# Four row slots a stage, rows addressed by byte offset and shared by SyncE and ScalarE, attribute loads issued by ScalarE

## The chip, the cores and the metric

The kernel runs on one core of a Trainium2 chip. The metric is device time in microseconds of one execution. The kernel before has a median of 3977.24 us in three runs (3971.26 to 3994.51).

## What is computed

The graph has 6250 nodes with 128 features, and 100000 directed edges sorted by target (`dst`). Two blocks follow each other, each added to its own input; each begins with a layer norm and a ReLU over the node features. The first block is two layers with edge attributes, the second two layers without:

```
h = relu(layernorm(x))                         # before each block
# block 1, two layers:
msg = relu(x[src] + edge_attr)                 # 100000 x 128
agg = segment_sum(msg, dst)                    # 6250 x 128
h = (x + agg) @ W1 + b1;  h = batchnorm(h) * gamma + beta
x = relu(relu(h) @ W2 + b2)
# block 2, two layers:
agg = segment_sum(x[src], dst)
x = relu((x + agg) @ wA + bA) @ wB + bB        # relu between the layers
```

## The kernel before, in words

Edges are handled 512 at a time, 4 per partition (`EPP`); such a group is a slot. Four slots make a turn, 49 turns (`TURNS`) a pass over all edges. Each of the four layers is one pass, called a stage here. The change touches the first two stages, those with edge attributes, and leaves the other two alone.

In a turn of the first two stages:

- **GpSimd** gathers node rows. For each slot it issues 4 indirect DMAs (line 629), each of 128 rows of the node table in HBM into one of two gather buffers `xg`. It may fill a buffer again when VectorE has summed the slots of two turns ago.
- **SyncE** issues, in this order (`edges`, line 534): the stores of finished count units (line 538, after ScalarE's cast of the unit), then, once TensorE is done with the turn, the edge attributes of the turn three ahead (1 MB in two DMAs, lines 499 and 503, into a ring of three), then `gather_rows`.
- **`gather_rows`** (line 507) is a second way of fetching node rows. Slot 2 of turns 25 and 48 isn't gathered by GpSimd; its 512 rows are fetched singly by SyncE into the tile `row_slot`. Six partitions of 4 rows each, 24 rows, are fetched in a turn: turns 2 to 23 for the first of these slots, 26 to 47 for the second. A load of 4 indices into registers (line 520) is followed by 4 DMAs of one table row, 512 bytes (line 524), each with register operations for its address. The index is a row number.
- **ScalarE** copies one attribute slot at a time to a bank of PSUM, `ea_stage` (line 704), turns sums into messages with a ReLU, two slots at a time (line 709), and casts finished count units to `count_out` (line 696), two of which are in flight to HBM.
- **VectorE** adds the gathered rows to the staged attributes (`slot_sum`, line 1048), which frees the bank for ScalarE's next copy. Between these sums it builds one-hot rows of the chunks of edges to be counted (`cell_room`, line 1035), once a turn the one-hot windows of targets (`hid`, line 995), and it adds TensorE's window sums to `acc` (line 948).
- **TensorE** first builds the counts of the turn (line 1407) and then sums messages into windows, 32 matmuls a turn (line 1423), whose last one increments `scattered`.

The counts built in the first two stages serve the last two, which need no attributes. The order of all of it is written out by hand, each engine having its own program, in which it runs strictly in order; semaphores tie them. In the code, `layer` is the stage, `n` the turn over both stages (0 to 97), `u` the slot.

Of the kernel before, what the change touches and what calls it, by code (L numbers as in the profile page):

```python
# [14 lines left out]
BF16 = mybir.dt.bfloat16  # L15

P = 128
NODES = 6250
EDGES = 100000
D = 128  # L20
EPP = 4
# [4 lines left out]
SLOTS = 4  # L26
# [68 lines left out]
ROW_TURNS = (25, TURNS - 1)  # L95
ROW_STARTS = (2, 26)
ROW_STEP = 6
# [21 lines left out]
def units_in(chunks):  # L119

    return [UNIT_OF[e] for c in chunks for e in (2 * c, 2 * c + 1) if e + 1 in UNIT_END]

# [59 lines left out]
def gnn_kernel(nc, x, src, dst, edge_attr, W1, b1, gamma, beta, W2, b2,  # L182
               w1a, b1a, w1b, b1b, eps1, w2a, b2a, w2b, b2b, eps2, out):
    with ExitStack() as ctx:
# [102 lines left out]
        row_slot = sb("row_slot", [P, EPP * D])  # L287
        product = row_slot[:, 0:UPG * CW].rearrange("p (s c) -> p s c", s=UPG)
# [90 lines left out]
        gathered = [[sem(f"gathered{q}_{u}") for u in range(SLOTS)] for q in range(2)]  # L379
        row_landed = [sem(f"row_landed{k}") for k in range(len(ROW_TURNS))]  # L380
# [48 lines left out]
        def load_plan(eng):  # L429

            eng.wait_ge(plan_ready, 2)
            return (eng.value_load(plan_i[0:1, 1:2], min_val=0, max_val=SKIP),
                    eng.value_load(plan_i[0:1, 2:3], min_val=LEFT_PAIRS, max_val=TURNS // 2),
                    eng.value_load(plan_i[0:1, 3:4], min_val=0, max_val=1))

# [24 lines left out]
        def _(sp):  # L460
# [32 lines left out]

            def load_turn(n):

                k, t = n % TURNS, n % RING
                e0 = k * SLOTS * SUP
                most = SLOTS - 1
                sp.dma_start(ea[:, t, 0:most, :, :].rearrange("p u j d -> p u (j d)"),  # L499
                             edge_attr[e0:e0 + most * SUP, :].rearrange("(u p j) d -> p u (j d)", p=P, j=EPP)  # L500
                             ).then_inc(ea_loaded[t], 16)
                e1 = min(e0 + most * SUP, TAIL_START)
                sp.dma_start(ea[:, t, most, :, :].rearrange("p j d -> p (j d)"),  # L503
                             edge_attr[e1:e1 + SUP, :].rearrange("(p j) d -> p (j d)", j=EPP)
                             ).then_inc(ea_loaded[t], 16)

            def gather_rows(layer, t):

                for k, (first, used) in enumerate(zip(ROW_STARTS, ROW_TURNS)):
                    p0 = (t - first) * ROW_STEP  # L510
                    if not 0 <= p0 < P:
                        continue
                    if t == first:
                        sp.wait_ge(table_written, 16 * GROUPS * (layer + 1))
                        if layer or k:
                            last = (layer * TURNS + ROW_TURNS[k - 1] - (0 if k else TURNS)) * SLOTS + ROW_SLOT
                            sp.wait_ge(summed, last + 1)
                    s = used * SLOTS + ROW_SLOT
# [15 lines left out]
            def edges(layer):  # L534
                for n in range(layer * TURNS, (layer + 1) * TURNS):
# [32 lines left out]
            rounds = load_rounds(sp)  # L568
            edges(0)
# [91 lines left out]
        def _(act):  # L661
# [36 lines left out]

            def stage_attributes(i):

                n, u = divmod(i, SLOTS)
                if u == 0:
                    act.wait_ge(ea_loaded[n % RING], 32 * (n // RING + 1))
                act.copy(ea_stage, ea[:, n % RING, u, :, :].rearrange("p j d -> p (j d)")).then_inc(ea_staged, 1)  # L704

# [5 lines left out]
            def edges(layer):  # L711
                start = RAW_TURNS if layer == 0 else layer * TURNS
                for n in range(layer * TURNS, start):
                    for slots in HALVES:
                        act.wait_ge(summed, n * SLOTS + slots[-1] + 1)
                        messages(n, slots)
                act.wait_ge(windows_cleared, 2 * (layer + 1))
                stage_attributes(start * SLOTS)
                for n in range(start, (layer + 1) * TURNS):
                    for slots in HALVES:  # L720
                        for u in slots:
# [4 lines left out]
                            if u == slots[-1]:  # L726
                                messages(n, slots)
                            units_out(slot_chunks(n, u))

# [108 lines left out]
            act.wait_ge(params_loaded, PARAMS)  # L838
            for layer in range(LAYERS):
                if layer < 2:  # L840
                    edges(layer)
                else:
                    if layer == 2:
                        rounds = load_rounds(act)
# [10 lines left out]
        def _(dve):  # L855
# [183 lines left out]
            def slot_sum(n, u):  # L1039
# [3 lines left out]
                if by_rows(n, u):  # L1043
                    k, rows = ROW_TURNS.index(n % TURNS), row_slot[:, :]
# [583 lines left out]
```

## Time and profile before

| | |
|---|---|
| median of 3 runs | 3977.24 us |
| profiled execution, own time | 4016.24 us |
| its span | 4014.3 us |
| granted TensorE clock, mean | 0.733 |
| busy share: TensorE, VectorE, ScalarE, GpSimd | 53%, 42%, 18%, 48% |
| first stage, turns 5 to 48 by SyncE's count | about 163 to 1509 us |
| second stage, row turns | about 1687 to 2958 us |
| third and fourth stage | about 3045 to 4014 us |

The span is that of the instructions; the execution's own time has 2 us more around it. A busy share is an average over stages with different limits. A wait that ends by "issue" is one in which the engine waited for nothing that the profile shows. "remote" is a releaser that the profile could not name.

### The profile page before, as it was taken

To read this page: it belongs to the slowest core of one execution; us is meant where nothing else is said; L and a number is where in the kernel's file an instruction comes from. 1 tells how busy PE (TensorE), PEld (TensorE's weight loads), DVE (VectorE), ACT (ScalarE), POOL (GpSimd) and SP (SyncE) were. 2 spreads that over 40 slices of the span, in tenths; PEclk is the share of its full clock that TensorE was granted. 3 is DMA by queue.
4 is the path that set the end of the run, shared out by engine and by line. 5 is a ranking of instruction groups with operands and counts; after the bars stand their busy time and mean duration, and the time that the engine had idled before them with its cause. 6 is when DMAs were issued, how large, how long until landed. Compare 5 with 4: busy or idle time off the path is not lost.

```text
span 4014.3 us, 37448 instructions
## 1 busy us (share of the span) xinstructions
PE 2131.0 (53%) x9399; PEld 1315.4 (33%) x9399; DVE 1694.4 (42%) x2879; ACT 732.8 (18%) x1002; POOL 1944.6 (48%) x2048
## 2 busy tenths in 40 slices
PE   2454544444444454344434454353456887877878
PEld 1332323332232232222222232232233444444445
DVE  6554435445454443445445554444456111151112
ACT  3111112121111123122112222222234000020001
POOL 5555445455453523655554554455423455445552
PEclk8676666766666677666766776666767898888889
DMA  4222222222222232232332323333323444443442
GB/s 141 72 74 76 84 62 79 78 89 82 73 81 74 82 89 84 75 89 82 101 100 87 108 90 108 91 93 97 113 83 106 151 147 134 132 143 124 151 148 83
DMA packets 228500, 396.97 MB, mean 99 GB/s; under 512 B 43017, under 2 KB 132957, under 8 KB 228325
## 3 DMA queue, kind: packets, MB, share of 16 engines
q1 hardware_dynamic: 163300, 261.77, 19.8%
q0 software_dynamic: 65024, 133.30, 13.0%
q8 instruction: 57, 0.93, 0.1%
q14 instruction: 119, 0.97, 0.1%
HBM read 333.10 MB, written 61.81 MB: 98 GB/s over the span
## 4 chain that ended last, share of the span: by engine, by line
SPq 38%; issue 30%; PE 21%; another core or an unknown queue 6%; DVE 4%; ACT 1%; DMA 0%; DVEq 0%; ACTq 0%
SPq L524 28%; PE psA L1450 13%; SPq L520 6%; PE psG L1465 4%; SPq L503 1%; PE psG L1514 1%; SPq L499 1%; PE psG L1423 1%; SPq L538 1%; PE psA L1522 1%; DVE cell_room L1035 0%; DVE rows_h L902 0%; PE psA L1407 0%; PE psG L1544 0%
## 5 line engine op out<-in xcount | busy, mean ns | idle before, releaser
L629 POOL DMA_INDIRECT xg<-node_table,src_all x1520 | 1441.7, 948 | 1457.7 <-DVE xp_room L1048 891.0
L1407 PE MATMUL psA<-cell_room,xp_room 128*128 128x512 f16 (+1 forms) x2336 | 705.8, 452 | 1061.9 <-ACT count_out L696 621.0
L1423 PE MATMUL psG<-hid,xp_room 128*128 128x160 f32 x3072 | 582.5, 352 | 487.4 <-issue 278.9
L1035 DVE TENSOR_SCALAR cell_room<-psG,cell_all 128x932 f16<-128x932 int16 x1088 | 686.5, 690 | 199.9 <-remote 158.0
L1407 PEld LDWEIGHTS psA<-cell_room,xp_room 128*128 128x128 f16 x2336 | 258.9, 115 | 1492.2 <-issue 682.1
L1048 DVE TENSOR_TENSOR xp_room<-psG,xg 128x512 f32<-128x512 f32 x380 | 258.0, 679 | 1117.7 <-ACT psG L704 992.3
L649 POOL DMA_INDIRECT xg<-node_table,idx x480 | 469.0, 977 | 535.3 <-issue 380.2
L1423 PEld LDWEIGHTS psG<-hid,xp_room 128*128 128x128 f32 x3072 | 547.1, 233 | 520.1 <-issue 380.8
L704 ACT COPY psG<-xp_room 128x512 f32<-128x512 f32 x384 | 226.5, 590 | 1230.5 <-DMA xp_room<-in_edge_attr_dram 627.2
L696 ACT CAST count_out<-psA 128x1862 f16<-128x1862 f32 x96 | 164.2, 1710 | 1061.2 <-DMA count_store<-count_out 444.1
L1450 PE MATMUL psA<-cell_room,xp_room 128*128 128x456 f16 x1200 | 275.2, 383 | 99.6 <-issue 77.7
L948 DVE TENSOR_TENSOR acc<-acc,row_slot 128x38 f32 x192 | 38.6, 201 | 632.7 <-ACT row_slot L756 526.7
L995 DVE SCALAR_TENSOR_TENSOR hid<-loc_all,round_off,psG 128x2560 f32<-128x2560 f32 x96 | 274.7, 2861 | 0.0
L1450 PE MATMUL psA<-hid,xp_room 128*128 128x456 f16 x1152 | 240.2, 368 | 15.0 <-issue 15.0
L1465 PE MATMUL psG<-rows_h,xg 128*128 128x160 f32 x960 | 193.7, 356 | 80.4 <-issue 80.3
L1465 PEld LDWEIGHTS psG<-rows_h,xg 128*128 128x128 f32 x960 | 177.2, 236 | 101.3 <-issue 99.2
L709 ACT ACTIVATE xp_room<-xp_room 128x1024 f32<-128x1024 f32 x196 | 206.2, 1053 | 9.7 <-issue 7.2
L1450 PEld LDWEIGHTS psA<-cell_room,xp_room 128*128 128x128 bf16 x1200 | 120.7, 101 | 246.6 <-issue 145.3
L948 DVE TENSOR_TENSOR acc<-acc,psG 128x160 f32 x272 | 86.9, 319 | 185.5 <-issue 89.9
L756 ACT COPY row_slot<-psA 128x456 f32<-128x456 f32 x16 | 8.6, 539 | 831.9 <-remote 695.0
L1450 PEld LDWEIGHTS psA<-hid,xp_room 128*128 128x128 bf16 x1152 | 112.3, 98 | 138.3 <-issue 22.6
L1014 DVE TENSOR_TENSOR xp_room<-psG,src_lo_all 128x768 f16<-128x768 int16 (+2 forms) x132 | 93.2, 727 | 0.0
(154 smaller groups left out, 824.4 us busy)
## 6 DMA issues: line engine op xcount, KB each, us to landing
xp_room<-in_edge_attr_dram SPq DMA_DIRECT2D x98, 768.0 KB
cell_room<-count_store SPq DMA_DIRECT2D x16, 2850.0 KB
count_store<-count_out SPq DMA_DIRECT2D x96, 465.5 KB
hid<-count_store SPq DMA_DIRECT2D x16, 2736.0 KB
row_slot<-node_table SPq DMA_DIRECT2D x2048, 0.5 KB
xp_room<-in_edge_attr_dram SPq DMA_DIRECT2D x98, 256.0 KB
xg<-node_table,src_all POOLq DMA_INDIRECT x1520
node_table<-rows_h SPq DMA_DIRECT2D x48, 256.0 KB
```

Source lines behind the costliest of these rows:

```text
L520: _, rows = nc.values_load_multi_w_load_instructions(src_all[p:p + 1, s, :], [mybir.EngineType.SP], min_val=0, max_val=NODES - 1, skip_run ...
L524: sp.dma_start(row_slot[p:p + 1, j * D:(j + 1) * D], table[bass.DynSlice(row, 1), :]).then_inc(row_landed[k], 16)
L629: nc.gpsimd.indirect_dma_start(xg[:, n % 2, u, j, :], None, x if n < RAW_TURNS else table, bass.IndirectOffsetOnAxis(ap=src_all[:, s, j:j ...
L649: nc.gpsimd.indirect_dma_start(xg[:, q, u, j, :], None, table, bass.IndirectOffsetOnAxis(ap=idx[:, q, u, j:j + 1], axis=0),).then_inc(row_ ...
L704: act.copy(ea_stage, ea[:, n % RING, u, :, :].rearrange("p j d -> p (j d)")).then_inc(ea_staged, 1)
L995: nc.vector.scalar_tensor_tensor(out=rows.rearrange("p u j w -> p (u j) w"), in0=loc.unsqueeze(2).broadcast_to((P, SLOTS * EPP, WIN)), sca ...
L1035: nc.vector.tensor_scalar(cells[:, c % CELL_RING, c0:c1], iota_bank[:, 0:c1 - c0], float(c0), cell_all[:, c:c + 1], ALU.add, ALU.is_equal) ...
L1048: nc.vector.tensor_tensor(ea[:, n % RING, u, :, :].rearrange("p j d -> p (j d)"), ea_stage, rows, ALU.add).then_inc(summed, 1)
L1407: last = nc.tensor.matmul(psA[:, bank, 0:w], src_hot[:, hots(n) % 2, at, :], cells[:, c % CELL_RING, c0:c0 + w], start=first, stop=end)
L1423: last = nc.tensor.matmul(psG[:, q, h * WIN:(h + 1) * WIN], ea[:, t, u, j, :], rows[:, u, j, :], start=(u == slots[0] and j == 0), stop=(u ...
L1450: last = nc.tensor.matmul(out_cols, xp[:, b, part, :], counts[h][:, :, i * CW:(i + 1) * CW], start=(b == 0 and part == 0), stop=(b == BLOC ...
L1465: last = nc.tensor.matmul(psG[:, q, h * WIN:(h + 1) * WIN], xg[:, q, u, j, :], late_hot[:, q, u * EPP + j, :], start=(u == slots[0] and j ...
```

## The change

- Four slots of each of the first two stages come row by row: slot 2 of turns 15, 26, 37 and 48. They go alternately into `row_slot` and into the last 512 columns of `hid`, which the one-hot windows don't reach.
- The 512 partition groups of 4 rows are worked off at 12 groups a turn, from turn 3 on: 8 groups (32 rows) by SyncE, 4 groups (16 rows) by ScalarE.
- The indices of these slots are loaded once, at the start, into the tile `idx` (free until the third stage), and shifted left by 9 bits by VectorE: they are byte offsets into the table, which is viewed as bytes. One index load of SyncE covers up to 4 groups (16 values), one of ScalarE 2 groups (8 values).
- ScalarE loads indices behind slots 0 and 2 of a turn and issues 4 rows behind each of the four slots.
- The attribute load of turn n + 2 (the ring's next) is issued by ScalarE, behind slot 1 of turn n and its first messages, after a wait for TensorE's windows of turn n - 1. SyncE no longer waits for TensorE in these stages.

```diff
-ROW_TURNS = (25, TURNS - 1)
-ROW_STARTS = (2, 26)
-ROW_STEP = 6
+ROW_TURNS = (15, 26, 37, TURNS - 1)
+ROW_START = 3
+BY_SYNC = 8
+ACT_GROUPS = ((1, 1), (1, 1))
+BY_ACT = sum(map(sum, ACT_GROUPS))
+ROW_STEP = BY_SYNC + BY_ACT
+ROW_LOAD = 4
...
+def row_work(t):
+    first = (t - ROW_START) * ROW_STEP
+    return [divmod(i, P) for i in range(first, first + ROW_STEP) if 0 <= i < len(ROW_TURNS) * P]
...
+def row_runs(work, most):
+    runs = []
+    for k, p in work:
+        if runs and runs[-1][0] == k and p % 8 and runs[-1][2] < most:
+            runs[-1][2] += 1
+        else:
+            runs.append([k, p, 1])
+    return runs
...
+        row_slots = [row_slot[:, :], hid[:, PADDED - EPP * D:PADDED]]
...
+        def row_bytes(offset):
+            return table.rearrange("(o n) d -> o (n d)", o=1).bitcast(U8)[:, bass.DynSlice(offset, ROW_BYTES)]
...
             def gather_rows(layer, t):
-                for k, (first, used) in enumerate(zip(ROW_STARTS, ROW_TURNS)):
...
-                    for p in range(p0, min(p0 + ROW_STEP, P)):
-                        _, rows = nc.values_load_multi_w_load_instructions(
-                            src_all[p:p + 1, s, :], [mybir.EngineType.SP], min_val=0, max_val=NODES - 1,
-                            skip_runtime_bounds_check_because="the load checks its address against the table itself")
-                        for j, row in enumerate(rows):
-                            sp.dma_start(row_slot[p:p + 1, j * D:(j + 1) * D],
-                                         table[bass.DynSlice(row, 1), :]).then_inc(row_landed[k], 16)
+                for k, p, groups in row_runs(row_work(t)[0:BY_SYNC], ROW_LOAD):
+                    if p < ROW_STEP:
                         sp.wait_ge(table_written, 16 * GROUPS * (layer + 1))
+                        sp.wait_ge(summed, buffer_free(layer, k))
+                    _, rows = nc.values_load_multi_w_load_instructions(
+                        row_list(k, p, groups), [mybir.EngineType.SP], min_val=0, max_val=(NODES - 1) * ROW_BYTES,
+                        skip_runtime_bounds_check_because="the load checks its address against the table itself")
+                    for i, row in enumerate(rows):
+                        r, j = p + i // EPP, i % EPP
+                        sp.dma_start(row_slots[row_buffer(layer, k)][r:r + 1, j * D:(j + 1) * D].bitcast(U8),
+                                     row_bytes(row)).then_inc(row_landed[k], 16)
...
-                    if n + RING < EDGE_TURNS:
-
-                        sp.wait_ge(scattered[n % 2], sp.snap(rounds * (n // 2 + 1) + 1))
-                        load_turn(n + RING)
                     gather_rows(layer, n % TURNS)
...
+            def load_behind(n):
+                if n < 0 or n + RING >= EDGE_TURNS:
+                    return
+                act.wait_ge(scattered[n % 2], act.snap(rounds * (n // 2 + 1) + 1))
+                t, slots, last = attributes_of(n + RING)
+                act.dma_start(ea[:, t, 0:SLOTS - 1, :, :].rearrange("p u j d -> p u (j d)"), slots).then_inc(ea_loaded[t], 16)
+                act.dma_start(ea[:, t, SLOTS - 1, :, :].rearrange("p j d -> p (j d)"), last).then_inc(ea_loaded[t], 16)
...
+            def gather_rows(layer, n, u):
+                half, second = divmod(u, 2)
+                at = BY_SYNC + sum(map(sum, ACT_GROUPS[:half]))
+                most = sum(ACT_GROUPS[half])
+                if not second:
+                    loaded.clear()
+                    for k, p, groups in row_runs(row_work(n % TURNS)[at:at + most], most):
...
+                        loaded.extend((k, p + i // EPP, i % EPP, row) for i, row in enumerate(rows))
+                first = ACT_GROUPS[half][0] * EPP
+                for k, r, j, row in loaded[first:] if second else loaded[:first]:
+                    act.dma_start(row_slots[row_buffer(layer, k)][r:r + 1, j * D:(j + 1) * D].bitcast(U8),
+                                  row_bytes(row)).then_inc(row_landed[k], 16)
...
                             if u == slots[-1]:
                                 messages(n, slots)
+                            if u == (SLOTS - 1 if n == RAW_TURNS else 1):
+                                load_behind(n - 1)
                             units_out(slot_chunks(n, u))
+                            gather_rows(layer, n, u)
...
+            dve.wait_ge(rows_listed, 16 * len(ROW_TURNS))
+            listed = idx[0:16 * len(ROW_TURNS), :, :, :].rearrange("p q u j -> p (q u j)")
+            nc.vector.tensor_scalar(listed, listed, ROW_BYTES.bit_length() - 1, None, ALU.logical_shift_left
+                                    ).then_inc(rows_scaled, 1)
```

## Rows read from the trace of the kernel before

**Rows 1.** The chain of waits, share of the span, first line of the page's part 4.

```profile
SPq 38%; issue 30%; PE 21%; another core or an unknown queue 6%; DVE 4%; ACT 1%; DMA 0%; DVEq 0%; ACTq 0%
```

**Rows 2.** The list of waits: engine and line, releaser, us in total, times, longest.

```profile
DVE xp_room L1048 <- ACT psG L704: 992.3, 77, 31.9
...
ACT psG L704 <- DMA xp_room<-in_edge_attr_dram: 627.2, 34, 39.6
```

**Rows 3.** The list of waits of the first stage, 163 to 1509 us.

```profile
ACT psG L704 <- DMA xp_room<-in_edge_attr_dram: 551.9, 31, 38.7
```

**Rows 4.** The list of waits of the second stage, 1687 to 2958 us.

```profile
ACT count_out L696 <- DMA count_store<-count_out: 404.3, 23, 28.0
```

**Rows 5.** Timeline of SyncE's queue, 597 to 662 us: start, us, what, count.

```profile
597.80 0.42 SPq L499 DMA_DIRECT2D xp_room<-in_edge_attr_dram  x1
...
613.37 0.41 SPq L499 DMA_DIRECT2D xp_room<-in_edge_attr_dram  x1
...
615.02 45.73 SPq L524 DMA_DIRECT2D row_slot<-node_table  x24
```

**Rows 6.** Timeline of SyncE's queue: attribute loads that bound four runs of turns.

```profile
162.98 0.37 SPq L499 DMA_DIRECT2D xp_room<-in_edge_attr_dram  x1
...
832.83 0.42 SPq L499 DMA_DIRECT2D xp_room<-in_edge_attr_dram  x1
...
838.96 0.41 SPq L499 DMA_DIRECT2D xp_room<-in_edge_attr_dram  x1
...
881.64 0.38 SPq L499 DMA_DIRECT2D xp_room<-in_edge_attr_dram  x1
...
1687.31 0.37 SPq L499 DMA_DIRECT2D xp_room<-in_edge_attr_dram  x1
...
2297.90 0.40 SPq L499 DMA_DIRECT2D xp_room<-in_edge_attr_dram  x1
...
2324.62 0.41 SPq L499 DMA_DIRECT2D xp_room<-in_edge_attr_dram  x1
...
2378.10 0.38 SPq L499 DMA_DIRECT2D xp_room<-in_edge_attr_dram  x1
```

**Rows 7.** Line 524 in 598 to 613.4 us: count, ns min/median/max, first and last start.

```profile
L524 SPq FUSED_REGOPS  x24: 3/37/37, 599.8 to 612.6; - x24
L524 SPq MOVE row_slot<-node_table x24: 3/29/29, 599.9 to 613.3; - x24
L524 SPq DMA_DIRECT2D row_slot<-node_table x24: 2/228/379, 600.0 to 613.3; - x24
```

**Rows 8.** Index loads: line 520 in 598 to 613.4 us, and line 433 of one value.

```profile
L520 SPq TENSOR_LOAD <-src_all x6: 559/562/699, 599.1 to 610.6; - x6
...
L433 SPq TENSOR_LOAD <-plan_i x1: 272/272/272, 2996.8 to 2996.8; - x1
```

**Rows 9.** Line 629 in 613.4 to 660.8 us.

```profile
L629 POOL DMA_INDIRECT xg<-node_table,src_all x29: 943/947/957, 612.9 to 648.2; - x29
```

**Rows 10.** Timelines of TensorE and VectorE in 620 to 639 us, with the idle before.

```profile
620.44 3.77 PE L1423 MATMUL psG<-hid,xp_room 128*128 128x160 f32 x26 [2.30 <-issue]
...
638.68 0.43 PE L1423 MATMUL psG<-hid,xp_room 128*128 128x160 f32 x1 [2.37 <-issue]
...
623.97 0.67 DVE L1048 TENSOR_TENSOR xp_room<-psG,xg 128x512 f32<-128x512 f32 x1
...
627.01 0.67 DVE L1048 TENSOR_TENSOR xp_room<-psG,xg 128x512 f32<-128x512 f32 x1
...
637.30 1.31 DVE L1035 TENSOR_SCALAR cell_room<-psG,cell_all 128x932 f16<-128x932 int16 x2 [8.41 <-remote]
```

**Rows 11.** Groups of instructions, page's part 5: count, busy us, mean ns, idle before.

```profile
L704 ACT COPY psG<-xp_room 128x512 f32<-128x512 f32 x384 | 226.5, 590 | 1230.5 <-DMA xp_room<-in_edge_attr_dram 627.2
L696 ACT CAST count_out<-psA 128x1862 f16<-128x1862 f32 x96 | 164.2, 1710 | 1061.2 <-DMA count_store<-count_out 444.1
...
L709 ACT ACTIVATE xp_room<-xp_room 128x1024 f32<-128x1024 f32 x196 | 206.2, 1053 | 9.7 <-issue 7.2
```

More of the change, by code:

```diff
@@ L15 @@
 BF16 = mybir.dt.bfloat16
+U8 = mybir.dt.uint8
 P = 128
@@ L20 @@
 D = 128
+ROW_BYTES = 4 * D
 EPP = 4
@@ L121, in units_in, with row_buffer, buffer_free @@
     return [UNIT_OF[e] for c in chunks for e in (2 * c, 2 * c + 1) if e + 1 in UNIT_END]
+def row_work(t):
[9 more added lines that the diff above has]
+    return runs
+def row_buffer(layer, k):
+    return (layer * len(ROW_TURNS) + k) % 2
+def buffer_free(layer, k):
+    i = layer * len(ROW_TURNS) + k - 2
+    if i >= 0:
+        return (i // len(ROW_TURNS) * TURNS + ROW_TURNS[i % len(ROW_TURNS)]) * SLOTS + ROW_SLOT + 1
+    return (RAW_TURNS + 2) * SLOTS if k else 0
 def by_rows(n, u):
@@ L434, in load_plan, with attributes_of, row_list @@
                     eng.value_load(plan_i[0:1, 3:4], min_val=0, max_val=1))
+        def attributes_of(n):
+            e0 = n % TURNS * SLOTS * SUP
+            e1 = min(e0 + (SLOTS - 1) * SUP, TAIL_START)
+            return (n % RING,
+                    edge_attr[e0:e0 + (SLOTS - 1) * SUP, :].rearrange("(u p j) d -> p u (j d)", p=P, j=EPP),
+                    edge_attr[e1:e1 + SUP, :].rearrange("(p j) d -> p (j d)", j=EPP))
+        def row_bytes(offset):
+            return table.rearrange("(o n) d -> o (n d)", o=1).bitcast(U8)[:, bass.DynSlice(offset, ROW_BYTES)]
+        def row_list(k, p, n):
+            part, at = 16 * k + p // 8, p % 8 * EPP
+            return idx[part:part + 1, :, :, :].rearrange("p q u j -> p (q u j)")[:, at:at + n * EPP]
         def uses_before(layer, q, pairs):
@@ L498, in load_turn @@
[L498 to L505, printed above, removed]
@@ L568, in _ @@
             rounds = load_rounds(sp)
+            sp.wait_ge(rows_scaled, 1)
             edges(0)
@@ L704, in stage_attributes @@
                 act.copy(ea_stage, ea[:, n % RING, u, :, :].rearrange("p j d -> p (j d)")).then_inc(ea_staged, 1)
+            loaded = []
+            def gather_rows(layer, n, u):
[5 more added lines that the diff above has]
+                    for k, p, groups in row_runs(row_work(n % TURNS)[at:at + most], most):
+                        if p < ROW_STEP:
+                            act.wait_ge(table_written, 16 * GROUPS * (layer + 1))
+                            act.wait_ge(summed, buffer_free(layer, k))
+                        _, rows = nc.values_load_multi_w_load_instructions(
+                            row_list(k, p, groups), [mybir.EngineType.Activation], min_val=0, max_val=(NODES - 1) * ROW_BYTES,
+                            skip_runtime_bounds_check_because="the load checks its address against the table itself")
+                        loaded.extend((k, p + i // EPP, i % EPP, row) for i, row in enumerate(rows))
[3 more added lines that the diff above has]
+                                  row_bytes(row)).then_inc(row_landed[k], 16)
             def messages(n, slots):
@@ L1043, in slot_sum @@
                 if by_rows(n, u):
-                    k, rows = ROW_TURNS.index(n % TURNS), row_slot[:, :]
+                    k = ROW_TURNS.index(n % TURNS)
+                    rows = row_slots[row_buffer(n // TURNS, k)]
                     dve.wait_ge(row_landed[k], 16 * SUP * (n // TURNS + 1))
```

23 lines of the change are left out of this document (12 added, 11 removed).

## The prediction

> **What bounds the kernel now.** I read the chain of waits first. It lies on the queue of SyncE for 38% of the span, nearly all of it in line 524, the single-row loads, and line 520, the index loads that feed them [rows 1]. The list of waits says what the other engines are doing meanwhile: VectorE waits 992 us for ScalarE's copy of an attribute slot, and ScalarE 627 us for the attribute load [rows 2]. Cut by stage, ScalarE waits 552 us for attributes in the first stage [rows 3], and 404 us in the second for a store of counts [rows 4]. Both of these transfers are issued by SyncE, behind the 24 rows of the turn before. So the question of every turn is how long SyncE takes for its rows.
>
> The timeline of SyncE answers it. 24 rows took from 599.1 us, the first index load [rows 8], to 613.37, 14.3 us, and the next 24 took 45.73 us; the attribute load went out at once when the rows were through [rows 5]. What differs is GpSimd: in the long turn it issued 29 indirect gathers back to back, from 612.9 to 648.2 us, one in 35.3 / 28 = 1.26 us [rows 9]. In the short one each row is three records, a fused register operation of 37 ns, a move of 29 ns and the DMA of 228 ns [rows 7], and every fourth row has an index load of 562 ns [rows 8]. The short turn lasts 15.6 us, the next 45.73 + 1.65 = 47.4 us. TensorE crawls in the same stretch: 26 matmuls from 620.44 us, then about one in 2.8 us, still at 638.68 us [rows 10]. Two prices then: with GpSimd quiet a row costs 14.3 / 24 = 0.59 us, index loads included; with GpSimd gathering 45.73 / 24 = 1.90 us.
>
> This gives the turn. A pair of turns has 31.7 indirect gathers (16 a turn, less 4 for each of the two turns of 49 whose slot 2 comes by rows), at 1.26 us 39.9 us with GpSimd on. In these SyncE gets 39.9 / 1.90 = 21 rows out, the other 27 cost 0.59 us, 15.9 us, and the attribute loads and stores some 3.6 us (1.65 us from one load's start to the next row in [rows 5]): 59.4 us, 29.6 a turn. From the first and the last of 21 turns in the first stage, and of 21 in the second, I read (669.9 + 610.6) / 42 = 30.5 us [rows 6]. The 0.9 us that is missing I keep as it is. Turns with no rows took 21.3 us (two in the first stage) and 26.7 us (two in the second), 24.0 in the mean [rows 6]: what is left when SyncE isn't the bound.
>
> **The change, part by part.** Row turns go from 44 to 43 a stage (512 groups of four rows at 12 a turn).
>
> *Rows by byte offset, SyncE.* 32 rows a turn instead of 24. The index load covers four groups, so two loads of 16 values replace six of four. The trace has no load of 16; one value takes 272 ns, four take 562 [rows 8], so 97 ns for each further one, 1.73 us for 16 (0.11 us a row, where now it is 0.14 and its gap). The upper bound is 16 single loads, 4.35 us. The shift by 512 leaves the address arithmetic; of three records a row one, two or three can remain. I take two: the fused operation is the arithmetic, and the move puts the result in its place. Records a row, index load included, fall from 3.25 to 2.06. If a row beside the gathers is paid by the record, it falls from 1.90 to 1.20 us; with GpSimd quiet from 0.59 to 0.48 (37 ns and its gap off, 0.04 us less index load). Ends: 0.62 us and 1.79 us beside the gathers, for one and for three records.
>
> *Four slots instead of two.* Eight gathers fewer a stage, 16 in all: 31.3 in a pair, 39.5 us with GpSimd on. On their own they are worth 16 x 1.26 = 20 us where GpSimd sets the end; here it is in the sum.
>
> *Attribute loads leave SyncE.* It keeps only the store, some 0.5 us a turn.
>
> *Sum.* Pair: 39.5 us, in which 33 rows go out; 31 at 0.48, 14.9; 1.0 for the stores: 55.4, 27.7 a turn, with the 0.9 us 28.6. Against 30.5 this is 1.9 us x 86 turns = 163 us; two turns lose their rows altogether, 2 x 6.5 = 13 us.
>
> *What ScalarE takes on.* Its copies (590 ns), messages (1053 ns) and casts (1710 ns) [rows 11] leave it idle most of a turn, but it stands in a ping-pong with VectorE, which adds a slot every 3.04 us (623.97 to 627.01 [rows 10]). Four rows a slot at 0.48 are 1.9 us, with the copy 2.5: hidden behind VectorE's 2.5 us of cells and its sum. At 1.20 us they are 4.8, and a slot takes longer than VectorE. The attribute load waits, behind slot 1 of a turn, for TensorE's windows of the turn before, and everything of ScalarE is queued behind it: the copy of slot 3, its messages, the cast that frees the counts' banks. In the pair shown it would have come to that wait after the sum of 623.97 (0.67 us), a copy and a message, at 626.3, and stood there beyond 639 us; but VectorE stood still too, 8.41 us for TensorE's use of the cells [rows 10], so most of it has cover. Ends: nothing, and the whole 13 us in every second turn (6.5 x 86 = 560 us). I take 0.3 us a turn, 26 us, near the low end, because the idle of VectorE has the same cause. The new waits on the shifted list, four small loads and one VectorE operation at the start cost below 2 us. The waits for a free buffer look back two slots, many turns.
>
> Total: -163 - 13 + 26 = -150 us on the profiled execution's own 4016.2: 3866. The median of the runs is 0.990 of it (3977.2), which gives 3830 us.
>
> One rule speaks against the wide index load. The Trainium skill, page "Runtime: NRT & Kernel Launch", section "Instruction fetch mechanics", puts a register load at about 200 ns a register, even in bulk. The rows, 272 ns for one value and 562 for four, are below that for each further value. By the page's figure 16 values are an estimated 3.2 us, a quiet row 0.57 instead of 0.48 us, and the whole change comes out at an estimated -30 us, hardly more than nothing. Rival 4 is the same mechanism, worked out from the rows.
>
> **The rivals.**
> 1. *One record a row.* The offset register goes straight into the DMA. Beside the gathers a row is 0.62 us, all 64 rows of a pair fit under the 39.5 us, and SyncE is no bound any more. For it: a byte offset needs no arithmetic. Then the row-free turn is the floor; the slower of the two, 26.7 us, since the long run is the second stage's pattern: -3.8 x 86 - 13 + 26 = -314 us, 3670. With 24.0 us it would be 3440.
> 2. *ScalarE becomes the bound, slower.* Place: the slot, in which ScalarE's rows stand between VectorE's sum and the next copy. If they pay the price of SyncE's beside the gathers, a slot is 0.67 + 0.59 + 4 x 1.20 = 6.1 us in two thirds of the time and 3.2 in the rest, 5.1 in the mean, against 3.04. The short turn of 15.6 us, in which VectorE and ScalarE set the pace and not SyncE, grows by 4 x 2.1 = 8.2 us, by 0.9 for the attribute issue and by 13 us of wait for TensorE in two thirds of the time, 8.7: a turn is 33 us, +2.9 x 86 - 13 = +236, 4210 at full price, 4190 with some of the wait covered. It decides from about 0.8 us a row on ScalarE. Against it: no ScalarE instruction in the trace shows the slow pace, but it never issues at such density either.
> 3. *Three records stay, the byte offset does nothing, slower.* 22 rows beside the gathers, 42 at 0.555: 63.7 us a pair, 32.8 a turn, +198 - 13 + 26: 4190. This is also the case in which the change doesn't do what it says.
> 4. *The index load grows by the register.* 4.35 us for 16: a quiet row 0.64, 31.1 a turn, +52 - 13 + 26: 4040. At half of that growth the result is no change.
>
> **How the numbers follow.** Forecast 0.36, one record 0.24, ScalarE 0.18, three records 0.10, index load 0.12, of which 0.03 slower and 0.09 within the bound. No change means within 0.5%, about what a measurement of this kernel can tell. Faster 0.60, same 0.09, slower 0.31. The range: below, the middle between the row-free floor of 24.0 and that of 26.7 us, 3560. Above, two thirds of the way from the time before to rivals 2 and 3, 4110, which leaves out some 0.15 above and 0.05 below. Since both signs hold much, the forecast's own range is 3745 to 3880 (a row beside the gathers at 1.1 or 1.35 us).
>
> **What the profile of after would show.** Right: records on SyncE's row line of two kinds, x2752 each; 32 rows in about 15 us when GpSimd is quiet and 38 when not; index loads at 1.7 us; ScalarE's wait for attributes gone from the head of the list; GpSimd's gathers 1504 instead of 1520. Wrong: SyncE with gaps between its row blocks (then rival 1, or ScalarE sets the pace); VectorE's wait for ScalarE's copy larger than 992 us (rival 2); a fused operation still ahead of each row (rival 3). The forecast falls as a whole if the price of a row doesn't go by records but by something else that the gathers share with SyncE.

## The result, and the profile after

| | before | after |
|---|---|---|
| median | 3974.25 us (4 runs, 3965.82 to 3994.51) | 3824.36 us (4 runs, 3807.04 to 3836.80) |
| ratio | | 0.9613 [0.9559, 0.9667] |
| profiled execution, span | 4016.24 us, 4014.3 us | 3807.04 us, 3805.2 us |
| granted clock, mean | 0.733 | 0.743 |

The change is worth 150 us by the medians, and 3.9% by the ratio. The forecast was 3830 us, so the size is right; the way to it is only partly the forecast's, as the rows show. The two profiled executions lie 209 us apart, because that of the kernel before was slower than its four timed ones and that of the changed kernel its fastest.

The chain of waits on the page, by engine and by line; the first line answers to [rows 1].

```profile
SPq 39%; issue 31%; PE 21%; DVE 3%; another core or an unknown queue 3%; ACT 1%; POOL 1%; DMA 1%; ACTq 0%; DVEq 0%
SPq L572 32%; PE psA L1536 13%; SPq L567 6%; PE psG L1551 5%; PE psG L1600 1%; PE psG L1509 1%; SPq L586 1%; PE psA L1608 1%; POOL xg L674 1%; ACT rows_h L722 0%; PE psA L1493 0%; DVE hid L1246 0%; PE psG L1630 0%; PE psA L1617 0%
```

The list of waits after, which answers to [rows 2].

```profile
ACT psG L758 <- issue: 1141.3, 239, 23.3
DVE xp_room L1130 <- ACT psG L758: 963.0, 105, 42.5
POOL xg L674 <- DVE xp_room L1130: 742.6, 105, 23.5
```

ScalarE's wait for attributes (627 us in [rows 2]) is gone. Now 1141 us stand as "issue" ahead of the same copy, a releaser that the trace doesn't name; all the idle time ahead of that copy has grown from 1230.5 us [rows 11] to 1467.3. VectorE's wait for the copy has hardly moved (992 to 963 us). The time was relabelled more than removed. SyncE holds 39% of the chain, as before (38%).

All single rows of SyncE (line 572 is the old 524), with the index loads and GpSimd's gathers, over the whole span: count, ns min/median/max, first and last start. These answer to [rows 7] and [rows 8].

```profile
L572 SPq MOVE row_slot<-node_table x1376: 1/29/1403, 106.7 to 2459.9; - x197
L572 SPq DMA_DIRECT2D row_slot<-node_table x1376: 2/228/1467, 106.7 to 2459.9; - x197
L572 SPq MOVE hid<-node_table x1376: 2/29/1409, 491.9 to 2767.6; - x197
L572 SPq DMA_DIRECT2D hid<-node_table x1376: 1/228/1395, 492.0 to 2767.7; - x197
L567 SPq TENSOR_LOAD <-idx x172: 4/1254/4372, 105.7 to 2761.0; - x172
L674 POOL DMA_INDIRECT xg<-node_table,src_all x1504: 939/946/2327, 74.1 to 2753.9; - x188
```

The fused operation has left, move and DMA remain: two records a row, each 2 x 1376 = 2752 times. An index load of 16 values takes 1.25 us. SyncE doesn't rest. Its queue's own list of waits is empty from 240 to 1340 us and from 1667 to 2740 us, and its timeline behind a store of counts is one unbroken run of rows:

```profile
518.88 0.38 SPq L586 DMA_DIRECT2D count_store<-count_out  x1
522.28 77.23 SPq L572 DMA_DIRECT2D hid<-node_table  x80
```

**A turn.** The attribute load is issued once a turn, so the starts of loads 5 and 40 span 35 turns in the first stage, and the second row 35 turns in the second stage.

```profile
L750 ACTq DMA_DIRECT2D xp_room<-in_edge_attr_dram x36: 407/412/414, 240.7 to 1207.9; - x36
L750 ACTq DMA_DIRECT2D xp_room<-in_edge_attr_dram x36: 407/412/439, 1667.3 to 2632.6; - x36
```

(1207.9 - 240.7) / 35 = 27.6 us, and again 27.6, against 30.5 in [rows 6] and 28.6 forecast. The single turns say more. Here are ScalarE's attribute loads around the second slot that comes by rows.

```profile
707.41 0.41 ACTq L750 DMA_DIRECT2D xp_room<-in_edge_attr_dram  x1
734.53 0.41 ACTq L750 DMA_DIRECT2D xp_room<-in_edge_attr_dram  x1
749.74 0.41 ACTq L750 DMA_DIRECT2D xp_room<-in_edge_attr_dram  x1
782.34 0.41 ACTq L750 DMA_DIRECT2D xp_room<-in_edge_attr_dram  x1
821.45 0.41 ACTq L750 DMA_DIRECT2D xp_room<-in_edge_attr_dram  x1
```

An ordinary turn lasts 27 us, and nearly all of the first stage's do: the alternation of 15.6 and 47.4 us is gone. (In the second stage the turns are less even, with the same mean.) Around a slot of rows three turns take 15.2 + 32.6 + 39.1 = 86.9 us, 6 more than three ordinary ones. VectorE waits there for rows, as at the first such slot:

```profile
491.65 0.69 DVE L1130 TENSOR_TENSOR xp_room<-psG,row_slot 128x512 f32<-128x512 f32 x1 [14.64 <-DMA row_slot<-node_table]
```

What holds an ordinary turn at 27 us: ScalarE, TensorE and GpSimd in 556 to 577 us (start, us, what, count, idle before).

```profile
556.82 1.44 ACTq L779 DMA_DIRECT2D hid<-node_table  x4
...
559.56 1.05 ACT L785 ACTIVATE xp_room<-xp_room 128x1024 f32<-128x1024 f32 x1
572.64 0.41 ACTq L750 DMA_DIRECT2D xp_room<-in_edge_attr_dram  x1
...
573.70 1.71 ACT L741 CAST count_out<-psA 128x1862 f16<-128x1862 f32 x1 [13.09 <-issue]
573.77 1.31 ACTq L779 DMA_DIRECT2D hid<-node_table  x4
575.30 0.60 ACT L758 COPY psG<-xp_room 128x512 f32<-128x512 f32 x1
```

```profile
554.80 7.14 PE L1509 MATMUL psG<-hid,xp_room 128*128 128x160 f32 x32 [5.83 <-DVE hid L1076]
561.78 0.96 PE L1493 MATMUL psA<-cell_room,xp_room 128*128 128x512 f16 x4
575.46 3.01 PE L1493 MATMUL psA<-cell_room,xp_room 128*128 128x512 f16 x7 [12.72 <-ACT count_out L741]
```

```profile
568.58 0.94 POOL L674 DMA_INDIRECT xg<-node_table,src_all  x1 [0.30 <-issue]
576.89 0.94 POOL L674 DMA_INDIRECT xg<-node_table,src_all  x1 [7.37 <-DVE xp_room L1130]
```

ScalarE ends its messages at 560.6 and stands at the wait for TensorE's windows until 572.6, 12 us, with the cast behind it for which TensorE waits. Those windows, the 32 matmuls of line 1509, ended by TensorE's own records at 561.9, 10.7 us before the load; line 1493, which follows, is counts. (No record is missing: line 1509 has all its 3072.) The load goes out 4.06 us after the start of GpSimd's last gather. The other ordinary turns of the first stage are alike: the load goes out 10.0 to 13.4 us after the windows' end and 3.2 to 4.3 us after the start of the last gather. GpSimd resumes only when VectorE has added the next slot, which needs ScalarE's copy. That closes a loop: 18.8 us from the first to the last start of 16 gathers; 4.1 us to the release; 4.2 us for the loads, ScalarE's four rows, the copy and the sum, until the next gather starts at 576.9: 27.1 us.

Two limits stand side by side, then. The loop gives the ordinary turn its 27 us, in which SyncE gets some 28 of its 32 rows out; at a slot of rows everything waits until SyncE has made up what it lacks. Since SyncE never rests, its rows set the mean turn of 27.6 us.

### The profile page after: what moved, and what is told of

It reads as the page before. It is cut to its first block, busy times and chain, and to the rows that moved or that the text cites. A ratio compares the mean times of both kernels' runs of the same rounds, so it can differ in the third digit from the quotient of the medians.

```text
span 3805.2 us, 39344 instructions
## 1 busy us (share of the span) xinstructions
PE 2118.3 (56%) x9399; PEld 1287.6 (34%) x9399; DVE 1696.4 (45%) x2880; ACT 738.1 (19%) x1002; POOL 1929.6 (51%) x2032
## 4 chain that ended last, share of the span: by engine, by line
SPq 39%; issue 31%; PE 21%; DVE 3%; another core or an unknown queue 3%; ACT 1%; POOL 1%; DMA 1%; ACTq 0%; DVEq 0%
SPq L572 32%; PE psA L1536 13%; SPq L567 6%; PE psG L1551 5%; PE psG L1600 1%; PE psG L1509 1%; SPq L586 1%; PE psA L1608 1%; POOL xg L674 1%; ACT rows_h L722 0%; PE psA L1493 0%; DVE hid L1246 0%; PE psG L1630 0%; PE psA L1617 0%
## 5 line engine op out<-in xcount | busy, mean ns | idle before, releaser
L674 POOL DMA_INDIRECT xg<-node_table,src_all x1504 | 1426.0, 948 | 1273.8 <-DVE xp_room L1130 742.6
L1493 PE MATMUL psA<-cell_room,xp_room 128*128 128x512 f16 (+1 forms) x2336 | 749.3, 471 | 1060.4 <-issue 553.4
L1493 PEld LDWEIGHTS psA<-cell_room,xp_room 128*128 128x128 f16 x2336 | 268.6, 119 | 1510.4 <-issue 859.5
L1116 DVE TENSOR_SCALAR cell_room<-psG,cell_all 128x932 f16<-128x932 int16 x1088 | 684.6, 685 | 32.2 <-remote 30.5
L1509 PE MATMUL psG<-hid,xp_room 128*128 128x160 f32 x3072 | 529.5, 337 | 298.4 <-DVE hid L1076 178.2
L1509 PEld LDWEIGHTS psG<-hid,xp_room 128*128 128x128 f32 x3072 | 511.6, 222 | 329.1 <-issue 326.0
L758 ACT COPY psG<-xp_room 128x512 f32<-128x512 f32 x384 | 226.6, 590 | 1467.3 <-issue 1141.3
```

The costliest lines, as they stand in the source:

```text
L674: nc.gpsimd.indirect_dma_start(xg[:, n % 2, u, j, :], None, x if n < RAW_TURNS else table, bass.IndirectOffsetOnAxis(ap=src_all[:, s, j:j ...
L1116: nc.vector.tensor_scalar(cells[:, c % CELL_RING, c0:c1], iota_bank[:, 0:c1 - c0], float(c0), cell_all[:, c:c + 1], ALU.add, ALU.is_equal) ...
L1493: last = nc.tensor.matmul(psA[:, bank, 0:w], src_hot[:, hots(n) % 2, at, :], cells[:, c % CELL_RING, c0:c0 + w], start=first, stop=end)
L1509: last = nc.tensor.matmul(psG[:, q, h * WIN:(h + 1) * WIN], ea[:, t, u, j, :], rows[:, u, j, :], start=(u == slots[0] and j == 0), stop=(u ...
```

## The experiments

Ratios are against the kernel before, run beside each; diffs are against the changed kernel. The experiments met two machines (or two conditions of one; the runs don't tell which, and the same chip number, 9, stands in runs of both kinds). In the first four the kernel before took 4017.14 us (7 runs, 4003.20 to 4022.76), 1% more than above; in the other eight about 2764 us. A ratio holds only where it was taken.

**Row numbers again (4 slots, everything else of the change kept).**

```diff
-            return table.rearrange("(o n) d -> o (n d)", o=1).bitcast(U8)[:, bass.DynSlice(offset, ROW_BYTES)]
+            return table[bass.DynSlice(offset, 1), :]
...
-            nc.vector.tensor_scalar(listed, listed, ROW_BYTES.bit_length() - 1, None, ALU.logical_shift_left
+            nc.vector.tensor_scalar(listed, listed, 0, None, ALU.logical_shift_left
```

> The changed kernel with one part undone: rows are addressed by row number (the list is not shifted), so a row is three records again instead of two; sharing, slots and attribute loads stay. Theory RECORDS (SyncE's rows are paid by the record and set the pace): SyncE got 28 rows out in a turn of 27 us with two records; with three a turn of 32 rows takes about 33 us, the kernel 4150 to 4200 us. Rival RELEASE (in the changed kernel a turn is GpSimd's burst of 16 gathers, 20 us, then 4.0 us until TensorE's semaphore arrives, then 3 us of ScalarE and VectorE; SyncE is not the bound): 3824 us, within 1%, except that rows land later in the four turns that need them, at most +60 us.

Measured 4135.64 us, 1.0302 [1.0279, 1.0325]: slower than before, just under the 4150 that theory RECORDS named, and 250 us above the most that RELEASE allowed. The third record is back, and the mean turn is 31 us ((1312.9 - 241.4) / 35 = 30.6 in the first stage, 31.2 in the second). Its line 572, and its attribute loads around the second slot of rows:

```profile
L572 SPq FUSED_REGOPS  x2752: 1/37/1396, 108.0 to 3080.4; - x197
```

```profile
775.91 0.41 ACTq L750 DMA_DIRECT2D xp_room<-in_edge_attr_dram  x1
791.40 0.41 ACTq L750 DMA_DIRECT2D xp_room<-in_edge_attr_dram  x1
815.81 0.41 ACTq L750 DMA_DIRECT2D xp_room<-in_edge_attr_dram  x1
904.83 0.41 ACTq L750 DMA_DIRECT2D xp_room<-in_edge_attr_dram  x1
```

The ordinary turns of the first stage are 27 us here too. The loss is at the slots: 15.5 + 24.4 + 89.0 = 128.9 us, 48 above three ordinary turns instead of 6. The price of a row explains it. These are SyncE's rows beside one burst of 16 gathers, the 19.7 us from the start of the first to the end of the last, in the changed kernel and then in this one.

```profile
L572 SPq DMA_DIRECT2D row_slot<-node_table x15: 4/228/712, 406.7 to 424.0; - x15
```

```profile
L572 SPq DMA_DIRECT2D row_slot<-node_table x11: 6/225/708, 408.2 to 423.9; - x11
```

1.31 us a row with two records, 1.79 with three. From load to load that is 25 to 31 rows in an ordinary turn of the first stage, 28 in the mean, against 16 to 23, 20 in the mean; the turn's list has 32. One such turn of this kernel:

```profile
L572 SPq DMA_DIRECT2D row_slot<-node_table x20: 12/225/709, 932.4 to 959.1; - x20
```

Eleven turns of lag are worked off at the slot.

These prices are means over a burst; within it a row gets dearer. Counted from the starts of the rows in the first stage's bursts, index loads included, in us a row:

| time since the burst's first gather | 0 to 5 us | 5 to 10 | 10 to 15 | 15 to 20 |
|---|---|---|---|---|
| before, three records | 0.87 | 2.18 | 4.03 | 4.91 |
| row numbers again, three records | 0.84 | 2.07 | 3.24 | 4.30 |
| the changed kernel, two records | 0.61 | 1.39 | 2.30 | 2.56 |
| ScalarE's wait behind slot 3 (next experiment), two records | 0.69 | 1.39 | 2.33 | 2.66 |

At every point of the burst two records cost 0.60 to 0.73 of what three cost in the row-number kernel; by the count of records, index load included, it would be 2.06 / 3.06 = 0.67.

**ScalarE's wait behind slot 3 instead of slot 1.**

```diff
-                            if u == (SLOTS - 1 if n == RAW_TURNS else 1):
+                            if u == SLOTS - 1:
```

> The changed kernel with ScalarE's attribute load, and so its wait for TensorE's windows of the turn before, behind slot 3 instead of slot 1. Theory RELEASE: the copy of slot 3 no longer waits for TensorE's semaphore (sum 3 of a turn comes 14 us behind sum 2 now, 3 us then), GpSimd's buffer is free earlier, the turn falls from 27 to about 24 us: 3600 to 3700 us. Theory RECORDS: SyncE's 32 rows set the end anyway, what the copies gain comes back as longer waits for rows in turns 15, 26, 37 and 48: 3790 to 3840 us.

Measured 3868.45 us, 0.9625 [0.9604, 0.9646], the same as the change (0.9613). The 3600 to 3700 us of theory RELEASE is out; theory RECORDS named 3790 to 3840, for a kernel before that was 1% faster. The turns become irregular, and the idle goes elsewhere (its list of waits):

```profile
POOL xg L674 <- DVE xp_room L1130: 804.7, 84, 36.2
ACT psG L758 <- issue: 740.3, 202, 24.2
```

So the place of the wait alone isn't the bound: SyncE's rows stand right beside it. Here too SyncE's queue waits for nothing in the first stage but 0.3 us for one cast (240 to 1208 us), and more of GpSimd's bursts are of 24 gathers, in which the rows are dearest.

**No rows at all**: every slot by indirect gathers, 1536 in all; once in the kernel before, once in the changed one.

```diff
-    return [divmod(i, P) for i in range(first, first + ROW_STEP) if 0 <= i < len(ROW_TURNS) * P]
+    return []
...
-    return u == ROW_SLOT and n % TURNS in ROW_TURNS
+    return False
```

(In the kernel before, `by_rows` the same and `ROW_STARTS` beyond the last turn.)

> The kernel before without any single-row loads: GpSimd gathers all four slots of all turns (784 indirect gathers a stage instead of 776), attribute loads by SyncE as before. The output stays what it was. Theory RECORDS: SyncE is free, a turn falls from 30.5 to the 24.0 us of the row-free turns: 98 x -6 = about 3400 us. Rival: the turn of before was held by GpSimd's bursts of 28 gathers, in which TensorE's releases stand still, and rows only fitted in: 3900 to 4000 us.

> The changed kernel without any single-row loads: GpSimd gathers all slots (784 a stage), attribute loads by ScalarE behind slot 1. The output stays what it was. Theory RELEASE: the turn stays at 16 x 1.25 + 4.0 + 3 = 27 us, but the four long turns of 43 to 47 us a stage go (8 x -17 = -136 us), and 32 x 1.25 = 40 us of gathers come back: about 3720 us. Theory RECORDS: with SyncE free the turn falls to 24 us or below: 3450 to 3550 us.

Measured 3653.86 us, 0.9097 [0.9059, 0.9135], and 3619.07 us, 0.9012 [0.8993, 0.9030]. Each lies between the two theories that were set against each other (3400 and 3900; 3550 and 3720), so neither SyncE's rows nor the release is the whole of it. On this machine both beat the change, which pays more for its rows than its 32 gathers save. The first shows that the alternation of long and short turns isn't the rows' doing. It has none, its queue stands idle, and its attribute loads come after 6 and 42 us still:

```profile
372.68 0.38 SPq L499 DMA_DIRECT2D xp_room<-in_edge_attr_dram  x1
...
378.98 0.38 SPq L499 DMA_DIRECT2D xp_room<-in_edge_attr_dram  x1
...
421.33 0.38 SPq L499 DMA_DIRECT2D xp_room<-in_edge_attr_dram  x1
```

The second has no row in any queue either, and shows the release by itself (ScalarE, TensorE, GpSimd):

```profile
513.82 0.39 ACTq L750 DMA_DIRECT2D xp_room<-in_edge_attr_dram  x1
```

```profile
496.40 7.42 PE L1509 MATMUL psG<-hid,xp_room 128*128 128x160 f32 x32 [7.91 <-DVE hid L1076]
```

```profile
510.10 0.94 POOL L674 DMA_INDIRECT xg<-node_table,src_all  x1 [0.30 <-issue]
516.37 0.94 POOL L674 DMA_INDIRECT xg<-node_table,src_all  x1 [5.32 <-DVE xp_room L1130]
```

Again the load goes out 3.7 us after the start of the last gather, and 10.0 us after the windows ended at 503.8. Its mean turn is (1128.4 - 236.0) / 35 = 25.5 us. From the load to the next burst it takes 2.55 us (513.82 to 516.37), where the changed kernel takes 4.25 (572.64 to 576.89): there ScalarE's four rows, 1.31 us, stand ahead of the copy. Of the changed kernel's 27.6 us the rows thus cost 2.1 in the mean: 1.5 in each ordinary turn, and these are ScalarE's rows, and the rest at the slots, for SyncE's.

**The parts one by one**: byte offsets and the wide load alone (attribute loads and 24 rows a turn stay with SyncE); attribute loads by ScalarE alone; the change with two slots.

```diff
-ROW_TURNS = (15, 26, 37, TURNS - 1)
+ROW_TURNS = (25, TURNS - 1)
...
-BY_SYNC = 8
-ACT_GROUPS = ((1, 1), (1, 1))
+BY_SYNC = 6
+ACT_GROUPS = ((0, 0), (0, 0))
...
+                    if n + RING < EDGE_TURNS:
+                        sp.wait_ge(scattered[n % 2], sp.snap(rounds * (n // 2 + 1) + 1))
+                        load_turn(n + RING)
...
-                if n < 0 or n + RING >= EDGE_TURNS:
-                    return
+                return
```

The second keeps `BY_SYNC = 6`, row numbers and index loads of four values, and leaves the last two edits out. The third has two slots with

```diff
-BY_SYNC = 8
-ACT_GROUPS = ((1, 1), (1, 1))
+BY_SYNC = 4
+ACT_GROUPS = ((1, 0), (1, 0))
```

> One part done alone, on the structure of the kernel before: two row slots, 24 rows a turn, all by SyncE, attribute loads by SyncE; only the addresses are byte offsets and an index load covers up to four groups. Theory RECORDS: rows cost the kernel before about 3.7 us a turn (29.7 against 26.0 without rows); with 2.1 to 2.3 records a row instead of 3.25 that is about 2.4, a turn of 28.4: ratio to before 0.96 to 0.975. Rival (what helped was that the attribute load left SyncE): 0.99 to 1.0.

> The other part alone: two row slots, 24 rows a turn by SyncE with row numbers (three records, index loads of four), but attribute loads by ScalarE behind slot 1. Theory RECORDS: SyncE still needs its 24 rows a turn but nothing waits behind them except the stores of counts: ratio 0.97 to 0.99. Theory RELEASE (ScalarE's wait closes the 27 us loop and nothing else binds): 0.92 to 0.95.

> The changed kernel with two row slots instead of four: 24 rows a turn, 16 by SyncE and 8 by ScalarE, all else as changed; GpSimd issues 16 gathers more. If the four slots are what gained, this is slower than 3824 us by up to 16 x 1.26 = 20 us and more. If rows cost more than the gathers that they save (theory ROWS COST: 48 rows a turn hold the changed kernel 1.9 us a turn above the one without), half of them costs half or less: 3640 to 3730 us, ratio 0.91 to 0.93.

**All 48 rows of a turn by SyncE.**

```diff
-BY_SYNC = 8
-ACT_GROUPS = ((1, 1), (1, 1))
+BY_SYNC = 12
+ACT_GROUPS = ((0, 0), (0, 0))
```

> The changed kernel with all 48 rows of a turn on SyncE, none on ScalarE. Theory RECORDS: SyncE gets 28 rows out in 27 us while GpSimd gathers for 20 of them, and the rest at 0.34 us each, so 48 rows take about 34 us: 4400 us or more. If ScalarE's share was a burden and not a help (it stands in the chain of the slots): below 3824 us.

These four met the other machine, where the kernel before took 2763.52 us. Measured: offsets alone 2753.69, 0.9971 [0.9959, 0.9982]; loads alone 2760.07, 0.9989 [0.9979, 0.9998]; two slots 2761.35, 0.9995 [0.9985, 1.0004]; all by SyncE 2844.63 (2 runs), 1.0298 [1.0277, 1.0319]. The numbers expected for all four failed, since they were made for the first machine. The reason is in SyncE's timeline of the first of them, beside a running burst of gathers:

```profile
516.58 8.61 SPq L572 DMA_DIRECT2D row_slot<-node_table  x24
```

0.36 us a row: the slow price isn't there, and with it goes what the byte offset had to give. The last of them shows the queue's limit here: 48 rows by SyncE make its queue 37% of the chain, and the kernel takes 3% more than before.

**The change itself on that machine, unaltered; the change without rows; and five slots with 60 rows a turn:**

```diff
-ROW_TURNS = (15, 26, 37, TURNS - 1)
+ROW_TURNS = (13, 22, 30, 39, TURNS - 1)
...
-BY_SYNC = 8
-ACT_GROUPS = ((1, 1), (1, 1))
+BY_SYNC = 10
+ACT_GROUPS = ((1, 1), (2, 1))
```

> The changed kernel, nothing altered, once more beside the kernel before. On the machine of the second set of experiments the kernel before takes 2763 us and a turn 19.8 us, which is 15.84 gathers at 1.25 us: there GpSimd's issue sets the end and SyncE's rows cost nothing. If this run meets such a machine: 16 gathers fewer, 20 us, ratio 0.993 (theory GPSIMD), or 1.00 to 1.03 if ScalarE's and SyncE's 48 rows a turn take it back (theory ROWS COST: the one with all 48 on SyncE took 1.030). If it meets one on which the kernel before takes some 4000 us: 0.961 again.

> The changed kernel without any single-row loads (GpSimd gathers all slots, 784 a stage) and with ScalarE's attribute load behind slot 3 instead of slot 1. Where the kernel before takes some 4000 us, theory RELEASE: the last wait for TensorE's semaphore leaves the chain of the copies, the turn falls from 25.6 us to about 23: 3400 to 3500 us, ratio 0.85 to 0.88; rival (GpSimd then gathers two turns at a stretch and TensorE's releases come later still): 0.90 to 0.92. Where it takes 2763 us, GpSimd's issue is the bound and its 16 gathers more than before cost 16 x 1.25 = 20 us: ratio 1.007.

> The changed kernel with five row slots a stage instead of four (turns 13, 22, 30, 39 and 48), 60 rows a turn: 40 by SyncE, 20 by ScalarE. GpSimd issues 8 gathers fewer than in the changed kernel, 24 fewer than before. Where the kernel before takes 2763 us, theory GPSIMD: 24 x 1.25 = 30 us, ratio 0.989, against 0.992 for four slots; rival (40 rows a turn are as much as SyncE can do beside the stores, as 48 were too many): 1.00 to 1.02. Where it takes some 4000 us, theory ROWS COST: 25% more rows cost more than 8 gathers: a turn above 28 us, ratio 0.98 to 1.02, against 0.961 for four.

> Byte offsets and the wide index load alone, once more (two row slots, 24 rows a turn and the attribute loads all on SyncE). Where the kernel before takes 2763 us: 0.997 again, since SyncE is not the bound there. Where it takes some 4000 us, theory RECORDS: rows cost the kernel before about 3.7 us a turn, with two records instead of three about 2.4: ratio 0.96 to 0.975; rival (the attribute load behind the rows is what held the turn): 0.99 to 1.0.

Measured: the change 2741.37 us, 0.9923 [0.9906, 0.9939]; without rows (the wait behind slot 3) 2783.62, 1.0077 [1.0060, 1.0094]; five slots 2733.65, 0.9893 [0.9877, 0.9908]; offsets alone again 2754.74, 0.9967 [0.9956, 0.9978]. Here all came as expected. The page of the changed kernel's run on this machine says why, in its chain by line:

```profile
POOL xg L674 49%; PE psA L1536 16%; PE psG L1551 4%; PE psG L1600 2%; PE psA L1608 1%; POOL xg L694 1%; DMA xg<-node_table,src_all 1%; DVE cell_room L1116 1%; PE psG L1509 0%; DVE xp_room L1130 0%; PE psG L1630 0%; DVE acc L1029 0%; DVE hid L1076 0%; DVE hid L1246 0%; PE psA L1617 0%
```

and its list of waits:

```profile
ACT psG L758 <- DVE xp_room L1130: 1073.4, 303, 16.6
...
POOL xg L674 <- issue: 465.7, 1527, 0.3
```

GpSimd issues without a pause (its idle is 0.3 us between gathers), so each gather saved is worth 1.25 us: 16 make 20 us of 2764, 0.7%, and 0.8% was measured. SyncE's queue does rest here: it waits 210 us for casts from 163 to 940 us. So the rows pay, and the kernel with five slots is the fastest of all that ran on this machine, 0.3% ahead of the change. On the first machine it wasn't run.

## Why the prediction was right, and where it wasn't

- **The price goes by the record: held, but the price isn't one number.** Two records a row as taken, and SyncE's rows beside the gathers 1.31 us (forecast 1.20), with three records 1.79 (1.90). Undoing this part alone turned 0.9613 into 1.0302, 7% of the time: it is worth more than the whole change, and what else the change does costs time without it. Rivals 1 (one record) and 3 (three stay) fall; rival 3's size for three records, 32.8 us a turn, was near the 31 measured. The forecast read its 1.90 from all 45.73 us of the long block, though GpSimd had stopped at 649.2 us. From 613.0 us to that end SyncE got only 10 rows out, some 3.6 us each, and 15 in the 12 us behind it:

```profile
L524 SPq DMA_DIRECT2D row_slot<-node_table x10: 2/691/708, 613.3 to 645.0; - x10
L524 SPq DMA_DIRECT2D row_slot<-node_table x15: 3/228/700, 649.1 to 660.5; - x15
```

  The price rises with the length of the burst (the table above), and the changed kernel's bursts are mostly of 16 gathers, where those before went up to 32. That a mean over burst and pause came near the price in a burst of 16 was luck.
- **Index load: held.** 1.25 us for 16 values, where 1.73 was taken and 4.35 was the bound; rival 4 falls. The estimate from the Trainium skill's figure, page "Runtime: NRT & Kernel Launch", section "Instruction fetch mechanics", was 3.2 us; the measurement decides against it here: the values come at (1254 - 562) / 12 = 58 ns each beyond the fourth. A quiet row still cost more than the 0.48 forecast: 12 rows in the 7 us between two bursts, 0.58.
- **ScalarE's rows, rival 2: fell, but they aren't free.** Four of them take 1.3 to 1.5 us, the changed kernel's first machine and a running burst included; 0.8 us each was the point from which it decides. The forecast had them hidden behind VectorE; the four behind slot 1 stand in the loop and make the ordinary turn 27 us. The changed kernel itself shows it in the two turns of the second stage that have no rows, 25.0 and 25.1 us.
- **ScalarE's wait: the step that failed.** "I take 0.3 us a turn" stood against ends of nothing and 13 us in every second turn. It is 12 us in the turn shown, and about as long in the other ordinary ones. The argument was that VectorE's standstill covers it, having the same cause; the runs show that VectorE stands still for this wait (11.46 us for ScalarE's copy at 575.9), and that it gives the ordinary turn its length. In the total it cost next to nothing all the same: with the wait moved (0.9625) the time is the same, because SyncE's rows would have to be waited for anyway. The small number was right for a reason that the forecast didn't give.
- **The sum: its bound was right in the mean.** The forecast had SyncE's rows as the bound of every turn, 27.7 us and 0.9 left over, 28.6; the mean is 27.6. (The left-over was 0.8: 59.4 / 2 is 29.7, not 29.6.) But it isn't the bound of each turn: ordinary turns last 27 us by the release, and the three around a slot take 6 to 8 us more than three ordinary ones. The forecast counted a row-free floor of 24 to 26.7 us ([rows 6]); the changed kernel without rows has 25.5, so the floor was right, and with it the reason that rival 1 had too much of the gain. The -150 us was worked out for the profiled execution, where the difference is 209 us; in the medians it is 150. That 3830 came within 6 us of 3824 is in part luck.
- **16 gathers fewer** and **ScalarE's wait for attributes gone**: both as said.

Open: what the attribute loads on ScalarE and its share of the rows give by themselves on the first machine, because those runs met the other one. That moving the wait gave nothing shows two bounds side by side; lifting both at once wasn't run there, except by taking the rows out. Nor was a version with ScalarE's rows out of the loop. What makes a row dearer the longer GpSimd gathers isn't known.

## What to carry to other kernels

Price a transfer by the records that it puts into its queue, not by its bytes: an address that is already a byte offset spares one of three here, and where that queue is the bound this was worth more than all else in the change. Read such a price by its place in the other engine's burst before averaging it: here it rose from 0.6 to 2.6 us a row within 20 us. Put what a cheap-looking helper path costs beside what it saves (512 single rows for four gathers, 5 us), and run the version without it: on one machine it was 6% faster than the changed kernel, on the other 1.5% slower (there with the wait behind slot 3). When a wait is moved to another engine, write down the whole loop that it closes; a wait that "has cover" can be what sets the length of a turn.

## What the runs showed of the hardware

- **The same kernel took 3974 us on one machine and 2764 us on another.** Both parts differ: in the changed kernel a turn of the first stage takes 27.6 against 19.2 us, and the last two stages, from their first gather on, 952 against 685 us. On the first, a SyncE record beside a burst of gathers often takes 0.7 us (maximum 712 ns in the rows above, median 228), on the other it doesn't (24 rows in 8.61 us). The mean granted clock is 0.73 to 0.76 in the first and 0.83 to 0.86 in the second. Why they differ isn't settled; only the kernel before and the changed one, run unaltered on both, allow the comparison.
- **On the first machine a row of SyncE gets dearer the longer GpSimd has been gathering**: with two records from 0.61 us in the first 5 us of a burst to 2.56 us from 15 us on, with three from 0.84 to 4.30; with GpSimd quiet it is 0.58.
- **On the first machine a release by TensorE arrives late, about 4 us after GpSimd's last gather** (4.06 and 3.72 us in the two turns shown), while the windows that it waits for end 10.7 and 10.0 us before the load by TensorE's records. Whether the semaphore is held up or the records are misplaced can't be told from the trace; the idle of ScalarE is real in either case. On the other machine this wasn't seen. There the changed kernel's load goes out 0.03 us after the windows' end, 539.78, in the middle of the gathers (ScalarE, then TensorE, then GpSimd):

```profile
539.81 0.41 ACTq L750 DMA_DIRECT2D xp_room<-in_edge_attr_dram  x1
```

```profile
532.66 7.12 PE L1509 MATMUL psG<-hid,xp_room 128*128 128x160 f32 x32 [8.55 <-DVE hid L1076]
```

```profile
539.64 0.94 POOL L674 DMA_INDIRECT xg<-node_table,src_all  x1 [0.30 <-issue]
```

- **ScalarE's rows stayed fast where SyncE's did not**: four in 1.44 us at 556.82, with a gather every 1.25 us beside them.
